# A transformer layer on one core: attention outputs turned by DMA instead of TensorE, output projection one segment later, residual rows loaded into the partial sums

## The chip, the core and the metric

The kernel runs on 1 core of one Trainium2 chip (trn2). The metric is the device time in microseconds (us). Times before: 3125.69 us, median of 3 runs (3119.35 to 3127.86).

## The reference

The input x is (16, 512, 256) in 32-bit floats: 16 batches of 512 tokens of width 256. One pre-norm layer is computed:

```python
def attn(inputs):                       # 32 query heads, 16 key/value heads, width 64
    qkv = inputs @ W_qkv                # 256 -> 2048 + 1024 + 1024
    scores = einsum('bhqd,bhkd->bhqk', q, repeat(k, 2)) / sqrt(64)
    scores = scores + alibi_slope[h] * (key_pos - query_pos)
    scores = where(causal, scores, -inf)
    out = einsum('bhqk,bhkd->bhqd', softmax(scores), repeat(v, 2))
    return out.reshape(B, S, 2048) @ W_out
def ffn(x):                             # 256 -> 64 -> 1024 -> 64 -> 256
    return (gelu((x @ U1) @ V1 + b1) @ U2) @ V2 + b2
x = x + attn(layernorm(x))
x = x + ffn(layernorm(x))
```

## The kernel before

**Numbers.** TensorE multiplies 16-bit floats, so nearly every operand is kept as two 16-bit halves: a high half (ScalarE rounds the value to 16 bits) and a low half (the rest, by VectorE where the value is in PSUM, by GpSimd where it is in SBUF). A product is three matmuls: low by high, high by low, high by high (`split_mm`, L437 through `mm`).

**Loops.** The outer loop runs over the 16 batches (`body(i, mode)`); the code of a body is written once for the first batch (FIRST), once as a hardware loop over the 15 others (MID), and once more as a tail (LAST) that finishes what is still in the pipe. A body has 16 steps `s`, one for each key/value head with its two query heads, and a step has 5 segments `n`. Each engine walks through the same steps and segments in a fixed order written by hand, and the engines are tied together by counting semaphores. The stages of a head are spread over several steps:

- step s: q of head s is projected (segment 1 or 2), k of a pair of heads in segment 0 of odd steps, v in segment 4 of steps 0 to 3 and 8 to 11. SyncE's DMA queue (SP) copies the halves to where the scores need them; `k_pair` copies are L394, L395 and L398, `q_pair` copies L406, L407 and L410.
- step s + 2: the row maxima of the scores, one block a segment (`max_scores` on TensorE, `maxima` on VectorE, L914). The key copies have to be there.
- step s + 7 (ATT): the scores again, one block a segment, transposed; ScalarE takes the exponential into `p_f` (L730, three buffers) and rounds it to `p_hi` (L688), GpSimd takes the low half `p_lo` (L1063). The high and low halves of segment n are made in segment n + 1, so those of segment 4 are made in segment 0 of the next step.
- step s + 8, segments 1 and 3: `attend`, the product with v for each of the two query heads into `o_acc`. The first waits for all five `p_lo` of the head. VectorE divides by the sum (`normalise`, L928 and L933) into `o_f`, 128 rows x (4 tiles x 128) in 32-bit floats.
- step s + 9, segment 0: `transpose_o`, four 128x128 transposes of `o_f` on TensorE into the PSUM bank `transposes` (L559). ScalarE rounds it into `ot[0]` (`o_t_hi`), VectorE takes `ot[1]` (`o_t_lo`, L837). `ot` is a ring of 8 heads.
- steps 12 to 15 and 0 to 11, segment 3 (OUT_SEG): `project_out`, 12 matmuls for one tile of 128 tokens and a group of 4 heads (a group takes 4 steps, one tile each). VectorE adds the result to `x_acc` (`add_out`, L921); the first group adds it to `x_residual`, the last one writes `x_rows`.
- steps 8 to 11: statistics of the second layer norm (L992 to L997, right after `add_out` in segment OUT_SEG), with the power on GpSimd (L1076) in segment 4; the feed-forward part follows up to step 15, its hidden layer in steps 13 and 14.
- after step 7, VectorE does the first layer norm of the next batch (`ln1`), with a power on GpSimd (L1046).

Projections share two PSUM banks in turn (`projection_order`, `next_proj`). SP's own order in a step: maxima (every fourth step), k copies (odd steps), q copies; the residual rows at s = 2, the next batch's rows at s = 4.

Of the kernel before, what the change touches and what calls it, by code (L numbers as in the profile page):

```python
# [28 lines left out]
P = 128  # L29
# [33 lines left out]
MAX_SEG, K_SEG, V_SEG = 1, 0, 4  # L63

OUT_RING, OUT_GROUP, OUT_LAG, OUT_SEG = 8, 4, 12, 3
# [83 lines left out]
MULTIPLES = (1, 2, 4, 8, 16, 32, 64, 80, 192)  # L149
# [60 lines left out]
def layer(nc, x, w_qkv, w_out, u1, v1, b1, u2, v2, b2, k_aug, q_aug, ident_d, ident_b_d, causal_d, out):  # L210
    B = x.shape[0]
    ctx = ExitStack()
    with ctx:
# [34 lines left out]
        o_f = sb("o_f32", [P, T, 2 * HD], F32)  # L248
        rden = sb("rden", [P, 2, T], F32)
        ot = [sb(f"o_t_{p}", [P, OUT_RING, S], F16) for p in ("hi", "lo")]  # L250
# [8 lines left out]
        xres = sb("x_residual", [P, T, D], F32)  # L259
# [25 lines left out]
        xres_in, y_out = sem("xres_in"), sem("y_out")  # L285
# [9 lines left out]
        hi_q, hi_k, hi_v, hi_ot, hi_m = sem("hi_q"), sem("hi_k"), sem("hi_v"), sem("hi_ot"), sem("hi_m")  # L295
# [4 lines left out]
        max_done, lo_q, lo_k, lo_v, lo_ot, lo_m = sem("max_done"), sem("lo_q"), sem("lo_k"), sem("lo_v"), sem("lo_ot"), sem("lo_m")  # L300
# [42 lines left out]
        def _(sp):  # L343
# [28 lines left out]
            def body(i, mode):  # L372
                for s in range(KV):
# [56 lines left out]
        def _(pe):  # L430
# [31 lines left out]
            def body(i, mode):  # L462
# [688 lines left out]
```

## Time and profile before

| | |
|---|---|
| median of 3 runs | 3125.69 us |
| profiled execution, its own time | 3124.16 us |
| its span, first to last instruction | 3122.4 us |
| TensorE (PE) busy | 2834.3 us, 91% |
| VectorE (DVE) busy | 2240.8 us, 72% |
| ScalarE (ACT) busy | 2167.0 us, 69% |
| GpSimd (POOL) busy | 1729.3 us, 55% |
| mean share of the DMA engines, all queues | 26.5% |
| mean granted TensorE clock | 0.987 |

One batch takes 188.6 us in the middle of the run: the scores of step 0 start at 1500.70 us and again at 1689.28 us. A matmul's busy time overlaps that of the next, so on TensorE the distance from one start to the next is what an instruction costs. In brackets at the end of a timeline row stands the idle time ahead of it and what ended it; "issue" is idle time that ended with nothing that the profile shows.

### The profile page before, as it was taken

To read this page: it belongs to the slowest core of one execution; us is meant where nothing else is said; L and a number is where in the kernel's file an instruction comes from. 1 tells how busy PE (TensorE), PEld (TensorE's weight loads), DVE (VectorE), ACT (ScalarE), POOL (GpSimd) and SP (SyncE) were. 2 spreads that over 40 slices of the span, in tenths; PEclk is the share of its full clock that TensorE was granted. 3 is DMA by queue.
4 is the path that set the end of the run, shared out by engine and by line. 5 is a ranking of instruction groups with operands and counts; after the bars stand their busy time and mean duration, and the time that the engine had idled before them with its cause. 6 is when DMAs were issued, how large, how long until landed. Compare 5 with 4: busy or idle time off the path is not lost.

```text
span 3122.4 us, 99572 instructions
## 1 busy us (share of the span) xinstructions
PE 2834.3 (91%) x32328; PEld 1975.6 (63%) x32328; DVE 2240.8 (72%) x7035; ACT 2167.0 (69%) x3828; POOL 1729.3 (55%) x1560
## 2 busy tenths in 40 slices
PE   4899999989989899899999999899898998999986
PEld 1576666766657566666766667666575666666664
DVE  6777677776767777677776777767677776777763
ACT  2676767667677676767767676676776767677683
POOL 1555555555555555555555555555555555555564
PEclk9999999999999999999999999999999999999997
DMA  6232232322223222232322323222232222323210
GB/s 167 64 72 55 56 73 48 79 53 64 62 54 77 48 67 60 56 74 46 78 54 55 74 47 78 54 63 62 54 77 48 67 60 56 74 48 78 55 36 8
DMA packets 220087, 195.25 MB, mean 63 GB/s; under 512 B 41738, under 2 KB 217866, under 8 KB 219274
## 3 DMA queue, kind: packets, MB, share of 16 engines
q1 hardware_dynamic: 219540, 188.32, 25.6%
q8 instruction: 299, 4.90, 0.7%
q14 instruction: 248, 2.03, 0.2%
HBM read 27.73 MB, written 8.39 MB: 12 GB/s over the span
## 4 chain that ended last, share of the span: by engine, by line
PE 30%; issue 28%; POOL 26%; ACT 5%; DVE 5%; POOLq 1%; DVEq 0%; ACTq 0%
POOL p_lo L1063 25%; PE proj L437 13%; PE scores L437 6%; PE o_acc L437 5%; PE max_scores L437 2%; PE ffn_acc L437 2%; ACT h_f L810 1%; ACT L730 1%; DVE max_scores L914 1%; DVE v_lo L837 1%; DVE x_rows L855 1%; ACT p_f L730 1%; ACT L810 1%; PE transposes L559 1%; POOL h_lo L1086 1%
## 5 line engine op out<-in xcount | busy, mean ns | idle before, releaser
L1063 POOL TENSOR_TENSOR p_lo<-p_f,p_hi 128x512 f16<-128x512 f32 x1280 | 1474.1, 1158 | 1103.1 <-ACT p_hi L688 1101.0
L730 ACT ACTIVATE p_f<-scores 128x512 f32<-128x512 f32 x1280 | 756.0, 591 | 432.3 <-PE scores L437 303.7
L688 ACT ACTIVATE p_hi<-p_f 128x512 f16<-128x512 f32 x1280 | 802.3, 627 | 53.4 <-issue 37.1
L914 DVE CUSTOM_DVE_ANT_0 max_scores<-max_scores,causal 128x384 f32<-128x384 f32 (+3 forms) x1184 | 564.2, 508 | 281.9 <-PE max_scores L437 279.5
L437 PE MATMUL scores<-q_hi_lo,k_lo_hi 128*128 128x512 f16 (+3 forms) x2048 | 614.7, 300 | 30.5 <-issue 30.2
L437 PE MATMUL scores<-q_hi_aug,k_hi_aug 128*128 128x512 f16 (+3 forms) x2048 | 587.4, 300 | 0.0
L437 PE MATMUL o_acc<-v_hi_one,p_lo 128*128 128x65 f16 x5120 | 521.3, 195 | 44.7 <-POOL p_lo L1063 44.6
L437 PEld LDWEIGHTS o_acc<-v_hi_one,p_lo 128*128 128x128 f16 x5120 | 473.7, 98 | 81.4 <-issue 42.3
L437 PE MATMUL o_acc<-v_lo,p_hi 128*128 128x64 f16 x5120 | 521.2, 194 | 0.0
L437 PE MATMUL o_acc<-v_hi_one,p_hi 128*128 128x65 f16 x5120 | 521.1, 195 | 0.0
L437 PEld LDWEIGHTS o_acc<-v_lo,p_hi 128*128 128x128 f16 x5120 | 470.5, 99 | 19.7
L437 PEld LDWEIGHTS o_acc<-v_hi_one,p_hi 128*128 128x128 f16 x5120 | 470.5, 98 | 0.0
L437 PE MATMUL scores<-ident_bf,causal 128*128 128x128 bf16 x2048 | 449.5, 220 | 0.0
L914 DVE CUSTOM_DVE_ANT_0 ffn_acc<-ffn_acc,causal 128x384 f32<-128x384 f32 (+2 forms) x864 | 413.9, 509 | 34.8 <-PE ffn_acc L437 33.6
L437 PE MATMUL max_scores<-k_hi_aug,q_hi_aug 96*128 96x384 f16 (+3 forms) x1184 | 284.0, 301 | 77.6 <-DVE row_max L914 74.1
L437 PE MATMUL proj<-xn_t_hi,wqkv_lo 128*128 128x512 f16 x768 | 294.4, 383 | 28.8 <-DVE v_lo L837 27.3
L437 PE MATMUL proj<-xn_t_lo,wqkv_hi 128*128 128x512 f16 x768 | 293.5, 382 | 0.0
L437 PE MATMUL proj<-xn_t_hi,wqkv_hi 128*128 128x512 f16 x768 | 293.3, 382 | 0.0
L437 PE MATMUL proj<-wo_hi,o_t_lo 128*128 128x256 f16 x1024 | 284.6, 278 | 2.6 <-DVE o_t_lo L837 1.5
L914 DVE DVE_READ_ACCUMULATOR2_ANT row_max<- 128x1 f32 x2048 | 284.8, 139 | 1.3
L437 PE MATMUL proj<-wo_hi,o_t_hi 128*128 128x256 f16 x1024 | 284.7, 278 | 0.0
L437 PE MATMUL proj<-wo_lo,o_t_hi 128*128 128x256 f16 x1024 | 284.2, 278 | 0.0
(110 smaller groups left out, 5212.0 us busy)
## 6 DMA issues: line engine op xcount, KB each, us to landing
q_hi_aug<-q_pair_hi SPq DMA_DIRECT2D x512, 64.0 KB, 2.0
q_hi_lo<-q_pair_hi SPq DMA_DIRECT2D x512, 64.0 KB, 2.0
q_hi_lo<-q_pair_lo SPq DMA_DIRECT2D x512, 64.0 KB, 2.0
k_hi_aug<-k_pair_hi SPq DMA_DIRECT2D x256, 64.0 KB, 2.0
k_lo_hi<-k_pair_hi SPq DMA_DIRECT2D x256, 64.0 KB, 2.0
k_lo_hi<-k_pair_lo SPq DMA_DIRECT2D x256, 64.0 KB, 2.0
x_rows<-in_L_attn_inputs SPq DMA_DIRECT2D x17, 512.0 KB, 3.8
x_residual<-in_L_attn_inputs SPq DMA_DIRECT2D x16, 512.0 KB, 3.8
```

Source lines behind the costliest of these rows:

```text
L437: return nc.tensor.matmul(out_ap, lhs, rhs, start=start, stop=stop, skip_group_check=True)
L559: last = nc.tensor.transpose(bank[:, qt * P:(qt + 1) * P], o_f[:, qt, :], ident[:, :])
L688: return nc.scalar.activation(out_ap, in_ap, ACT.Copy, scale=scale)
L730: nc.scalar.activation(p_f[:, k % 3, :], score_bank[k % 2][:, :], ACT.Exp).then_inc(exp_done, 1)
L810: nc.scalar.activation(h_f[:, c % 2, :], proj("h", c)[:, :], ACT.Gelu_apprx_tanh, bias=b1c[:, c:c + 1], scale=1.0 / FFN_SCALE).then_inc(ge ...
L837: return nc.vector.scalar_tensor_tensor(out=out_ap, in0=bank, scalar=scale, in1=high, op0=ALU.mult, op1=ALU.subtract)
L855: last = nc.vector.tensor_scalar(xt[:, t, :], xt[:, t, :], agg[:, t, 0:1], rstd[:, t:t + 1], ALU.subtract, ALU.mult)
L914: last = nc.vector.tensor_tensor_reduce(out=bank, in0=bank, in1=causal[:, (T - 1 - qt) * P:S], scale=1.0, scalar=-3e38, op0=ALU.add, op1=A ...
L1063: nc.gpsimd.tensor_tensor(p_lo[:, slot, n, :], p_f[:, k % 3, :], p_hi[:, slot, n, :], ALU.subtract).then_inc(lo_p, 1)
L1086: nc.gpsimd.tensor_tensor(h_lo[:, c % 2, :], h_f[:, c % 2, :], h_hi[:, c % 2, :], ALU.subtract).then_inc(lo_h, 1)
```

## The change

- `transpose_o` on TensorE, the rounding of its PSUM result (`o_t_hi`, ScalarE, step s + 9, segment 0) and the low half from PSUM (`o_t_lo`, VectorE) are gone.
- ScalarE now rounds `o_f` itself, before the transpose, into `o_hl[:, slot, 0]`, in step s + 8, segment 4 (O_SEG), after waiting for the second `normalise` of that step, which is in segment 3. `o_f` and `o_hl` have two slots.
- GpSimd takes the low half of `o_f` into `o_hl[:, slot, 1]` in step s + 9, segment 0, ahead of the `p_lo` of segment 4.
- SP issues one DMA transpose a head (128 rows x 1024 16-bit values, both halves) into `ot`. It stands in SP's list in step s + 8 after the q copies and waits for the low half, so SP gets past it in step s + 9. `project_out` waits for the DMAs of its group.
- `project_out` and `add_out`, with the layer-norm statistics behind them, move from segment 3 to segment 4.
- `x_residual` is gone. The residual rows are loaded straight into `x_acc`, in four DMAs of one tile each in steps 10 to 13, and the first `add_out` adds to `x_acc` in place.

```diff
-MAX_SEG, K_SEG, V_SEG = 1, 0, 4
+MAX_SEG, K_SEG, V_SEG, O_SEG = 1, 0, 4, 4
-OUT_RING, OUT_GROUP, OUT_LAG, OUT_SEG = 8, 4, 12, 3
+OUT_RING, OUT_GROUP, OUT_LAG, OUT_SEG = 8, 4, 12, 4
...
@@ SP
-                    if s == 2 and mode != LAST:
-                        if 16 * i - OUT_LAG > 0:
-                            sp.wait_ge(acc_done, at(16 * i - OUT_LAG))
-                        sp.dma_start(xres[:, :, :], x_src(i.value())).then_inc(xres_in, 16)
+                    if in_stage(mode, s, ATT + 1):
+                        slot, kv = s % 2, (s - ATT - 1) % KV
+                        sp.wait_ge(lo_o, at(g - ATT))
+                        sp.sem_inc(gate, 1)
+                        sp.dma_start_transpose(ot[:, kv % OUT_RING, :, :].rearrange("p a (t q) -> p (a t) q", q=P),
+                                               o_hl[:, slot, :, :].rearrange("p a q -> p (a q)")).then_inc(ot_in[slot], 16)
+                    if s in range(OUT_LAG - 2, OUT_LAG + 2) and mode != LAST:
+                        t = s - (OUT_LAG - 2)
+                        if 16 * i + t - 3 > 0:
+                            sp.wait_ge(acc_done, at(16 * i + t - 3))
+                        sp.dma_start(xacc[:, t, :], x_src(i.value())[:, t, :]).then_inc(xres_in[t], 16)
@@ TensorE
-                def transpose_o(s):
-                    a = i * KV + s - ATT - 2
-                    bank = transposes_bank(lo_ot, a + 1)
-                    pe.wait_ge(o_done, at(2 * (a + 1)))
-                    for qt in range(T):
-                        last = nc.tensor.transpose(bank[:, qt * P:(qt + 1) * P], o_f[:, qt, :], ident[:, :])
-                    last.then_inc(pe_ot, 1)
...
                     if t == 0:
-                        pe.wait_ge(lo_ot, at(16 * i + s - OUT_LAG + OUT_GROUP))
+                        for slot in range(2):
+                            pe.wait_ge(ot_in[slot], at(16 * (8 * i + (s - OUT_LAG) // 2 + 2)))
@@ ScalarE
-                        if n == out_segment(s) and in_stage(mode, s, ATT + 2):
-                            a = g - ATT - 2
-                            act.wait_ge(pe_ot, at(a + 1))
+                        if n == O_SEG and in_stage(mode, s, ATT + 1):
+                            a, slot = g - ATT - 1, s % 2
...
-                            copy(ot[0][:, a_slot(s) % OUT_RING, :], t_bank[:, :]).then_inc(hi_ot, 1)
+                            act.wait_ge(o_done, at(2 * (a + 1)))
+                            copy(o_hl[:, slot, 0, :], o_f[:, slot, :, :].rearrange("p t c -> p (t c)")).then_inc(hi_o, 1)
@@ VectorE
                     if h == 0:
-                        if a > 0:
-                            dve.wait_ge(pe_ot, at(a))
+                        if a > 1:
+                            dve.wait_ge(lo_o, at(a - 1))
...
-                        if n == out_segment(s) + out_lag(s) and in_stage(mode, s, ATT + 2):
-                            dve.wait_ge(hi_ot, at(g - ATT - 1))
-                            low(ot[1][:, a_slot(s) % OUT_RING, :], t_bank[:, :], ot[0][:, a_slot(s) % OUT_RING, :],
-                                1.0).then_inc(lo_ot, 1)
...
-                                if t == 0:
-                                    dve.wait_ge(xres_in, at(16 * (i + 1)))
-                                add_out(xacc, s, xres)
+                                dve.wait_ge(xres_in[t], at(16 * (i + 1)))
+                                add_out(xacc, s, xacc)
@@ GpSimd
                     for n in range(SEG):
+                        if n == 0 and in_stage(mode, s, ATT + 2):
+                            slot = (s - ATT - 2) % 2
+                            pool.wait_ge(hi_o, at(i * KV + s - ATT - 1))
+                            nc.gpsimd.tensor_tensor(o_hl[:, slot, 1, :], o_f[:, slot, :, :].rearrange("p t c -> p (t c)"),
+                                                    o_hl[:, slot, 0, :], ALU.subtract).then_inc(lo_o, 1)
                         if n > 0 and in_stage(mode, s, ATT):
                             low_p(SEG * (i * KV + s - ATT) + n - 1, s % 2, n - 1, SEG * s + n - 1)
```

## Rows read from the trace of the kernel before

**Rows 1.** The page: busy time of the engines.
```profile
PE 2834.3 (91%) x32328; PEld 1975.6 (63%) x32328; DVE 2240.8 (72%) x7035; ACT 2167.0 (69%) x3828; POOL 1729.3 (55%) x1560
```

**Rows 2.** TensorE's timeline in one batch: four of its 12 idle stretches.
```profile
1586.29 0.19 PE L437 MATMUL o_acc<-v_hi_one,p_lo 128*128 128x65 f16 x1 [2.36 <-POOL p_lo L1063]
...
1609.98 0.60 PE L530 MATMUL proj<-ident,row_max 128*8 128x128 f32 x4 [0.80 <-DVE v_lo L837]
...
1635.30 0.39 PE L437 MATMUL proj<-xn_t_hi,wqkv_lo 128*128 128x512 f16 x1 [0.51 <-DVE v_lo L837]
...
1689.28 0.39 PE L437 MATMUL scores<-q_hi_lo,k_lo_hi 128*128 128x512 f16 x1 [2.16 <-issue]
```

**Rows 3.** TensorE's timeline: the transposes of step 0 and the next block.
```profile
1501.42 0.60 PE L559 MATMUL transposes<-ident,o_f 128*128 128x128 f32 x4
1501.86 0.38 PE L437 MATMUL scores<-q_hi_lo,k_lo_hi 128*128 128x512 f16 x1
```

**Rows 4.** Groups by line: count, then busy us, mean ns of one, idle before.
```profile
L1063 POOL TENSOR_TENSOR p_lo<-p_f,p_hi 128x512 f16<-128x512 f32 x1280 | 1474.1, 1158 | 1103.1 <-ACT p_hi L688 1101.0
L688 ACT ACTIVATE p_hi<-p_f 128x512 f16<-128x512 f32 x1280 | 802.3, 627 | 53.4 <-issue 37.1
...
L837 DVE SCALAR_TENSOR_TENSOR o_t_lo<-transposes,o_t_hi 128x512 f16<-128x512 f32 x256 | 176.4, 689 | 49.5 <-ACT o_t_hi L688 39.4
...
L559 PE MATMUL transposes<-ident,o_f 128*128 128x128 f32 x1024 | 154.2, 273 | 1.5 <-DVE o_f L933 1.1 <-DVE xn_t_lo L837 0.4
...
L688 ACT ACTIVATE o_t_hi<-transposes 128x512 f16<-128x512 f32 x256 | 152.3, 595 | 7.2 <-PE transposes L559 7.2
```

**Rows 5.** Timeline, step 0 to 1: last `p_lo` and the `attend` behind it.
```profile
1512.07 1.16 POOL L1063 TENSOR_TENSOR p_lo<-p_f,p_hi 128x512 f16<-128x512 f32 x1 [2.83 <-ACT p_hi L688]
...
1513.74 0.20 PE L437 MATMUL o_acc<-v_hi_one,p_lo 128*128 128x65 f16 x1
```

**Rows 6.** TensorE's and GpSimd's timelines, steps 8 and 9.
```profile
1591.13 0.28 PE L437 MATMUL proj<-wo_hi,o_t_lo 128*128 128x256 f16 x1
1592.44 0.19 PE L437 MATMUL o_acc<-v_hi_one,p_lo 128*128 128x65 f16 x1
1593.35 0.27 PE L437 MATMUL scores<-q_hi_lo,k_lo_hi 128*128 128x256 f16 x1
1594.12 0.38 PE L437 MATMUL proj<-wqkv_hi,xn_t_lo 128*128 128x512 f16 x1
...
1594.91 0.54 POOL L1076 TENSOR_TENSOR rstd<-var_eps,nhalf 128x1 f32<-128x1 f32 x1 [1.78 <-DVE var_eps L997]
...
1598.57 0.20 PE L437 MATMUL o_acc<-v_hi_one,p_lo 128*128 128x65 f16 x1
```

**Rows 7.** The same two timelines, steps 14 and 15.
```profile
1662.91 0.60 PE L530 MATMUL proj<-ident,row_max 128*8 128x128 f32 x4 [0.55 <-ACT h_f L810]
...
1673.98 3.39 POOL L1063 TENSOR_TENSOR p_lo<-p_f,p_hi 128x512 f16<-128x512 f32 x3
...
1677.78 0.20 PE L437 MATMUL o_acc<-v_hi_one,p_lo 128*128 128x65 f16 x1
```

**Rows 8.** TensorE's timeline in the tail (LAST), one of seven alike.
```profile
3044.69 0.20 PE L437 MATMUL o_acc<-v_hi_one,p_lo 128*128 128x65 f16 x1 [1.17 <-POOL p_lo L1063]
```

**Rows 9.** DMA: the queue (packets, MB, share), issues (KB each, us to landing).
```profile
q1 hardware_dynamic: 219540, 188.32, 25.6%
...
q_hi_aug<-q_pair_hi SPq DMA_DIRECT2D x512, 64.0 KB, 2.0
...
x_residual<-in_L_attn_inputs SPq DMA_DIRECT2D x16, 512.0 KB, 3.8
```

**Rows 10.** Timelines, SP in step 5 and TensorE at the start of step 6.
```profile
1555.18 0.48 SPq L394 DMA_DIRECT2D k_hi_aug<-k_pair_hi  x1
...
1557.69 1.17 SPq L398 DMA_DIRECT2D k_lo_hi<-k_pair_lo  x2
...
1562.20 0.38 PE L437 MATMUL max_scores<-k_hi_aug,q_hi_aug 96*128 96x512 f16 x1
```

More of the change, by code:

```diff
@@ L146 @@
 PROJ = {use: k % 2 for k, use in enumerate(projection_order())}
-MULTIPLES = (1, 2, 4, 8, 16, 32, 64, 80, 192)
+MULTIPLES = (1, 2, 4, 8, 16, 32, 64, 80, 128, 192)
 FREE = 1
@@ L247, in layer @@
         p_lo = sb("p_lo", [P, 2, SEG, 512], F16)
-        o_f = sb("o_f32", [P, T, 2 * HD], F32)
+        o_f = sb("o_f32", [P, 2, T, 2 * HD], F32)
+        o_hl = sb("o_hi_lo", [P, 2, 2, S], F16)
         rden = sb("rden", [P, 2, T], F32)
-        ot = [sb(f"o_t_{p}", [P, OUT_RING, S], F16) for p in ("hi", "lo")]
+        ot = sb("o_t", [P, OUT_RING, 2, S], F16)
+        ot_half = [ot[:, half * OUT_RING // 2:(half + 1) * OUT_RING // 2, :, :] for half in range(2)]
+        staged_wo = [o.rearrange("p r a b -> p (r a b)").bitcast(F32).rearrange("p (c n) -> p c n", n=D) for o in ot_half]
         mcol = sb("row_max", [P, 2, T, 8], F32)
@@ L284, in layer @@
         zeroed, qaug_in, x_in, k_rows = sem("zeroed"), sem("qaug_in"), sem("x_in"), sem("k_rows_set")
-        xres_in, y_out = sem("xres_in"), sem("y_out")
+        xres_in, y_out = [sem(f"xres_in{t}") for t in range(T)], sem("y_out")
         qdup_in = [sem(f"qdup_in{r}") for r in range(RING)]
@@ L351, in _ @@
             for half in range(2):
-                sp.dma_start(ot[half][:, :, :].rearrange("p a b -> p (a b)").bitcast(F32).rearrange("p (c n) -> p c n", n=D),
+                sp.dma_start(staged_wo[half],
                              w_out[half * KV // 2 * P:(half + 1) * KV // 2 * P, :].rearrange("(c p) n -> p c n", p=P)).then_inc(w_in[2], 16)
@@ L581, in project_out @@
                     if t == 0:
-                        pe.wait_ge(lo_ot, at(16 * i + s - OUT_LAG + OUT_GROUP))
+                        for slot in range(2):
+                            pe.wait_ge(ot_in[slot], at(16 * (8 * i + (s - OUT_LAG) // 2 + 2)))
                     for k in range(OUT_GROUP):
                         kv = OUT_GROUP * group + k
-                        last = split_mm(bank[:, 0:D], [o[:, kv % OUT_RING, t * P:(t + 1) * P] for o in ot],
+                        last = split_mm(bank[:, 0:D], [ot[:, kv % OUT_RING, part, t * P:(t + 1) * P] for part in range(2)],
                                         [w[:, kv, :] for w in wo], k == 0, k == OUT_GROUP - 1)
@@ L704, in _ @@
             for half in range(2):
-                last = copy(wo[0][:, half * KV // 2:(half + 1) * KV // 2, :],
-                            ot[half][:, :, :].rearrange("p a b -> p (a b)").bitcast(F32).rearrange("p (c n) -> p c n", n=D), WO_SCALE)
+                last = copy(wo[0][:, half * KV // 2:(half + 1) * KV // 2, :], staged_wo[half], WO_SCALE)
             last.then_inc(split_hi, 1)
@@ L866, in _ @@
                 low(wqkv[1][:, c, :], src, wqkv[0][:, c, :], W_SCALE).then_inc(split_done, 1)
-            staged_wo = [o[:, :, :].rearrange("p a b -> p (a b)").bitcast(F32).rearrange("p (c n) -> p c n", n=D) for o in ot]
             small = p_hi[:, :, :, :].rearrange("p a b c -> p (a b c)").bitcast(F32)
@@ L929, in normalise @@
                     if h == 0:
-                        if a > 0:
-                            dve.wait_ge(pe_ot, at(a))
+                        if a > 1:
+                            dve.wait_ge(lo_o, at(a - 1))
                     dve.wait_ge(recip_done, at(2 * a + h + 1))
-                    nc.vector.tensor_tensor(o_f[:, :, h * HD:(h + 1) * HD], o[:, :, 0:HD],
+                    nc.vector.tensor_tensor(o_f[:, (s - ATT - 1) % 2, :, h * HD:(h + 1) * HD], o[:, :, 0:HD],
                                             rden[:, h, :].unsqueeze(2).to_broadcast([P, T, HD]),
```

23 lines of the change are left out of this document (9 added, 14 removed).

## The prediction

> **What bounds the kernel now.** I read the page first, then the groups by line, then TensorE's timeline through one batch, and last the timelines of the other engines at each place where TensorE's rows show idle time or come close to it. The page says that TensorE is busy 91% of the span and no other engine above 72% [rows 1]. The timeline says the same more sharply: in a batch of 188.58 us (the scores of step 0 to those of the next batch) TensorE's idle stretches are 12 rows with 13.9 us together, the first at 1586.29 and the last at 1689.28, and the rest is matmuls issued back to back [rows 2]. Three kinds of places matter here. Step 8 (2.36 us, and more behind it) is the first layer norm of the next batch. Steps 10, 11 and 12 each have a stall of 0.5 to 1.2 us for `v_lo`, of which the first and the last are shown. And 2.16 us go at the loop's end. So work taken from TensorE is worth its full issue time in most steps, and nothing in a step where a stall stands behind it.
>
> **What is removed.** Four transposes of `o_f` stand between two blocks for 1501.86 - 1501.42 = 0.44 us [rows 3]. (The group's busy time, 154 us for 1024, counts overlaps; the issue distance is 256 x 0.44 = 113 us.) In a batch that is 16 x 0.44 = 7.04 us. VectorE loses 256 x 0.689 = 176 us; ScalarE swaps a copy of 595 ns for one like `p_hi`, 627 ns; GpSimd gets 256 more of 1.16 us, 297 us or 65% busy in all [rows 4]. On none of the three is that a throughput limit; where it lies in the order is what counts.
>
> **Where the 0.44 us is not gained.**
>
> - Steps 10, 11, 12: the transposes stand ahead of a stall that ends with VectorE's `v_lo`, which hangs on the v projection and not on the transposes. The stall grows by what is taken away: -3 x 0.44 = -1.32. The `v_lo` chain itself I leave as long as it is: `add_out` and the statistics now come into it, but VectorE idled near there, and it loses `o_t_lo`.
> - Step 14: the stall ends with ScalarE's gelu [rows 7], whose queue holds the same work: -0.44.
> - Step 8: VectorE's `ln1` starts after `add_out` instead of before it, but segment 4 of step 7 starts 1.31 us earlier, since `project_out` follows it. I count the 0.44 as gained and 0.4 on top: +0.4.
> - Steps 1, 3 and 4: the last `p_lo` ends at 1513.23 and `attend` starts at 1513.74, 0.51 later [rows 5]. In step 8, where TensorE does wait, the start comes 0.23 after the end of `p_lo` (1584.90 + 1.16 = 1586.06 in the same timeline), so the slack is 0.28, and 0.16 of each 0.44 is lost: -0.5. The new low half of `o` doesn't add to it here: its input is there when segment 4's exponential is, and the v projection (1.3 us) and the moved `project_out` (1.31 us, 1591.13 to 1592.44 [rows 6]) run meanwhile. That is the cover; without it 1.16 us would be late in each step. In steps 5 to 7 the moved projection alone covers it, with some 0.2 us to spare by the same reckoning.
> - Step 9: GpSimd's power of the layer norm waits for VectorE's statistics, which now follow `project_out` in segment 4. Before, it starts 1594.91 - 1592.44 = 2.47 after the last output matmul. Now, from the start of the scores of segment 4: 0.77 (1593.35 to 1594.12) + 1.31 + 2.47 + 0.54 for the power, + 1.16 for the new low half, + 1.16 for the last `p_lo`, + 0.23 = 7.64. `attend` would be free to start after 5.22 (1593.35 to 1598.57) + 1.31 - 0.44 = 6.09 [rows 6]. Lost: -1.55. Steps 10 to 12 have at least 1.6 us more between the same two points and hide it.
> - Step 15: GpSimd comes out of the feed-forward low halves late and does three `p_lo` in a row, to 1677.37, and `attend` follows at 1677.78 [rows 7]. The new low half goes ahead of the third: `attend` starts at about 1677.37 + 1.16 + 0.23 = 1678.76, 0.98 later than before instead of 0.44 earlier: -1.42.
>
> Sum of a batch: 7.04 - 1.32 - 0.44 + 0.40 - 0.50 - 1.55 - 1.42 = 2.2 us. Some 15.5 batches have this cover (15 and steps 9 to 15 of the first): 34 us. In the tail nothing covers GpSimd: seven steps already wait 1.17 us for `p_lo` [rows 8], and each gets the rounding and the low half (0.6 + 1.16) less the 1.31 of `project_out` that now runs under them: I take +0.7 x 7 = +5. At the very end the last transpose is awaited by the last output projection, once: +3. Net -26.
>
> **The DMA transposes.** No row shows one. It moves 256 KB. Landing, from below: between 64 KB in 2.0 us and 512 KB in 3.8 us, so 2.8 us [rows 9]. The queue's packets take 25.6% x 16 x 3122.4 / 219540 = 58 ns each; if pieces are rows of 128 values (256 bytes), 1024 pieces take 1024 x 58 ns / 16 = 3.7 us of all engines; if they are 16 values long, 8192 take 30 us, the upper bound, which would fill the queue. I take 3.7 us, nearest to pieces like those the queue has now (1 KB rows), and about 5.5 us to landing. `project_out` needs it only in every fourth step, some 7 us or more after the low half. What else stands behind: SP's copies of k. In step 5 the first is issued at 1555.18 and the last ends issuing at 1558.86; it lands at 1560.9, and the maxima of step 6 start at 1562.20, so 1.3 us to spare; the transpose is issued some 1.8 us ahead of the first copy [rows 10]. So up to 3.1 us of issue, or 1.8 + 3.7 + 1.3 = 6.8 us in the rings, cost nothing. Issue of a copy is 0.6 us; eight such (one a block) would be 4.8 us and cost 1.7 us in steps 5 and 7, 16 batches: +54. I take one to three: 0.
>
> Here the Trainium skill speaks on both sides. Its page Advanced Engine Details and Errata, section X-Bar Transpose (TRN2), calls transposing DMAs as fast as ordinary ones; by that the price is 0, as above. No row here shows one.
>
> **Residual rows.** Four issues for one, 0.4 us each on SP, two steps (over 20 us) ahead of their use against a landing of 3.8 us or less [rows 9]; `add_out` costs the same in place. 0.
>
> **Forecast.** On the profiled execution's own 3124.16 us (span 3122.4), less 26: 3098. The median of the runs is 1.5 higher: 3099.
>
> **Rivals.**
>
> - *All of it is gained* (chance 0.12): the stalls above are shorter than I reckon since VectorE has 0.69 us a step less. 113 less 8 of the tail: 3125.7 - 105 = 3020. For it: many stalls end with VectorE. Against: steps 9 and 15 hang on GpSimd.
> - *GpSimd's new low half lies in the path* (0.13): VectorE gives `o_f` late, ScalarE, waiting for it in segment 4, is late with the rounding and with `p_hi` behind it, and GpSimd starts the new operation when it would have started the last `p_lo`. Then `attend` comes 1.16 - 0.28 = 0.88 later than before in 15 steps of 16 batches: +211, 3337. It decides from the point where more than 0.28 us of the 1.16 is exposed on the mean. For it: VectorE is at 72% and in bursts behind. Against: it loses 0.69 us a step, and the projection in segment 4 gives 1.31.
> - *The transposes fill the DMA queue* (0.11): the engines are 25.6% busy, 3.1 us of a 12.2 us step; a transpose of over 9.1 us makes them the bound. With pieces of 32 values, 4096 x 58 ns / 16 = 14.9 us, a step takes 14.9 + 3.1 = 18.0, and the kernel 256 x 18.0 + 60 for the ends = 4670; at 30 us, 8,500. For it: no row shows into how many pieces a transpose falls. Against: the row length of the data alone gives 3.7 us, and what stays under some 7 us costs nothing. It decides from there.
> - *Moved stalls eat all* (0.06): steps 0 to 7 lose their gain too, 3116 to 3135.
>
> The Trainium skill's page VectorE: DVE Perf Modes, section The three transpose paths, gives 1309 ns for a 128x128 block of 16-bit values by DMA. If eight such blocks add up, my estimate by that page is 10.5 us a transpose, the third rival's case at 256 x 13.6 + 60 = 3540; no row here shows it.
>
> **How the numbers follow.** The likeliest case has 0.58, with a range of its own of 3070 to 3120: the stalls of steps 9 and 15 may be absent (-47) or the small slacks of steps 5 to 7 gone (+20). About 0.3% (9 us) is what a measurement of this kernel can tell from no change. Faster: 0.54 + 0.12 = 0.66; same: 0.04 of the first case, 0.02 of the second rival's, 0.06 of the last: 0.12; slower: 0.11 + 0.11 = 0.22. The range reaches down to the first rival and up into the light cases of the second (less than half of the 1.16 us exposed): 3020 to 3150, with 0.01 left out below and 0.18 above.
>
> **What would show it.** The rows of L559, `o_t_hi` and `o_t_lo` are gone, and TensorE's busy time is down by some 110. Idle time ahead of `o_acc`, ended by `p_lo`, appears in steps 9 and 15 and not elsewhere. The transpose's row says its landing; wrong if above 7 us, or if TensorE waits for k copies or in `project_out` for a DMA. Wrong the other way if idle time in steps 10 to 12 doesn't grow. The second rival shows as idle time of TensorE before `o_acc` in nearly every step, with ScalarE waiting for `o_f`.

## The result

The kernel with the change takes 3190.22 us (median of 4 runs, 3179.89 to 3200.06) against 3123.95 us before (4 runs): ratio 1.0212, 95% interval 1.0174 to 1.0251. It is slower by 66 us, where 26 us less were forecast. Spans of the profiled executions: 3192.9 and 3122.4 us, mean granted clock 0.974 and 0.987.

The page of the kernel after, engines, queue and groups, answering to [rows 1, 4, 9]:

```profile
PE 2775.3 (87%) x31304; PEld 1868.7 (59%) x31304; DVE 2080.0 (65%) x6779; ACT 2183.6 (68%) x3828; POOL 2015.4 (63%) x1816
...
q1 hardware_dynamic: 490644, 255.46, 38.2%
...
L1046 POOL TENSOR_TENSOR p_lo<-p_f,p_hi 128x512 f16<-128x512 f32 x1280 | 1475.6, 1160 | 817.9 <-ACT p_hi L675 815.7
...
L1054 POOL TENSOR_TENSOR o_hi_lo<-o_f,o_hi_lo 128x512 f16<-128x512 f32 x256 | 295.6, 1155 | 14.1 <-ACT o_hi_lo L675 11.8
...
x_acc<-in_L_attn_inputs SPq DMA_DIRECT2D x64, 128.0 KB, 2.3
```

TensorE does less (2775 for 2834 us) in a longer span, so its idle time has grown. The view of waits (engine, line and tile that waited, what ended the wait; us in total, times, longest) says for what:

```profile
PE max_scores L433 <- DVE row_max L902: 80.6, 65, 2.7
PE o_acc L433 <- POOL p_lo L1046: 71.0, 38, 3.4
PE scores L433 <- issue: 50.4, 14, 4.8
PE proj L433 <- DVE v_lo L826: 41.4, 32, 1.7
PE proj L433 <- DVE x_acc L909: 39.8, 45, 1.1
```

In the kernel before, the same view has 74.1, 44.6, 30.2, 27.3 and 5.0 us. What stands out is the wait for `x_acc`, the sum that `add_out` writes: before, it was 0.34 us once a batch, in step 13. Another 9.4 us of it stand before the turning of the row maxima (L526). The loop's end ("issue") costs 20 us more, `p_lo` 26 us more. The transposes themselves are hardly to be seen: TensorE waits for one of them once in the whole run, 3.4 us.

Where in a batch it went. Step lengths (from one step's first scores to the next's), kernel after less kernel before. The measured column is one batch in the middle of each run (1528.36 to 1722.74 and 1500.70 to 1689.28), the last column the mean of the 14 batches from the first loop end to the tail:

| steps | forecast, us | measured, us | mean of 14, us |
|---|---|---|---|
| 0 | -0.44 | +1.21 | +1.22 |
| 1 to 4 | -1.28 | +2.22 | +2.22 |
| 5 to 7 | -1.32 | -1.31 | -1.34 |
| 8 | -0.84 | 0.00 | +0.18 |
| 9 | +1.11 | +0.24 | +0.24 |
| 10 to 12 | 0 | 0.00 | +0.36 |
| 13 | -0.44 | +0.10 | +0.10 |
| 14 | 0 | +0.73 | +0.73 |
| 15 | +0.98 | +2.61 | +1.30 |
| batch | -2.23 | +5.80 | +5.0 |

The one batch shown has the longest idle stretch of the run at its end (4.84 us in step 15, where the mean is 3.60), and no stretch at the low clock in steps 8 and 11, where some of the others have one.

Over the 14 batches the mean is 194.13 for 189.13, +5.0 us: 70 us. The tail got 3.4 us longer and the start 3.0 shorter, which makes the 70.5 us between the spans.

Steps 1 to 4. Timelines of TensorE and VectorE:

```profile
1541.46 0.39 PE L433 MATMUL proj<-xn_t_hi,wqkv_lo 128*128 128x512 f16 x1 [1.12 <-DVE x_acc L909]
...
1553.50 0.60 PE L526 MATMUL proj<-ident,row_max 128*8 128x128 f32 x4 [0.63 <-DVE x_acc L909]
```

```profile
1540.38 0.69 DVE L826 SCALAR_TENSOR_TENSOR v_lo<-proj,v_hi_one 128x512 f16<-128x512 f32 x1 [2.26 <-ACT v_hi_one L675]
1540.99 0.41 DVE L909 SCALAR_TENSOR_TENSOR x_acc<-proj,x_acc 128x256 f32<-128x256 f32 x1
```

In segment 4, VectorE does `v_lo` first and `add_out` behind it, though the matmuls of `project_out` ended before those of v. VectorE stands idle for 2.26 us until ScalarE has rounded v, so the PSUM bank of `project_out` comes free at 1541.4, and TensorE, which needs that bank for its next projection, waits 1.12 us. Before, `add_out` stood in segment 3.

Steps 15 and 0, the loop's end:

```profile
1716.66 0.27 PE L433 MATMUL proj<-v_hi,h_hi 128*128 128x256 f16 x1
1717.07 0.28 PE L433 MATMUL proj<-v_hi,h_lo 128*128 128x256 f16 x1
...
1717.63 0.27 PE L433 MATMUL proj<-v_hi,h_hi 128*128 128x256 f16 x1
1722.74 0.60 PE L433 MATMUL scores<-q_hi_lo,k_lo_hi 128*128 128x512 f16 x1 [4.84 <-issue]
```

```profile
1716.60 0.41 DVE L909 SCALAR_TENSOR_TENSOR x_acc<-proj,x_acc 128x256 f32<-128x256 f32 x1
```

`project_out` of step 15 stands directly ahead of the last projection of the feed-forward part (12 matmuls in two banks). Its second bank waits for `add_out`: 0.30 us at 1717.07. Then 4.84 us pass to the scores of the next body, 2.16 before [rows 2]. From the last projection's first matmul to the first scores the mean is 5.39 us, before 3.63; from there to the first `attend` 4.35 us, before 3.16 with 0.44 of transposes in it. The view by stretches shows why the second grew:

```profile
1718.00:1720.00 2.00, 0.00 (x0) 0.00 (x0) 0.63 (x1) 0.34 (x1) 1.15 (x1) 1.00 1.39 110
1720.00:1722.00 2.00, 0.00 (x0) 0.00 (x0) 0.00 (x0) 0.00 (x0) 0.00 (x0) 0.67 0.88 58
1722.00:1724.00 2.00, 1.26 (x4) 0.54 (x5) 0.00 (x0) 0.01 (x1) 0.00 (x0) 0.50 0.84 284
```

The columns are the stretch, its length, busy us of PE, PEld, DVE, ACT and POOL, then the granted clock, DMA share and GB/s. After the long idle stretch TensorE works at 0.50, the level of 1.2 GHz; before, the clock is 1.00 in every such stretch around 1689, and it is so behind all 14 ends. In the kernel after it falls to 0.50 at 13 of the 14 ends, at 9 of them only some matmuls behind the first scores, which still take 0.39 us. The batch before this one shows the fall; the same matmul takes 0.38 us at full clock:

```profile
1528.36 0.39 PE L433 MATMUL scores<-q_hi_lo,k_lo_hi 128*128 128x512 f16 x1 [3.28 <-issue]
...
1530.00 0.63 PE L433 MATMUL proj<-xn_t_hi,wqkv_lo 128*128 128x512 f16 x1
```

Steps 8 and 9. TensorE's waits and GpSimd's timeline in step 8:

```profile
1616.68 0.19 PE L433 MATMUL o_acc<-v_hi_one,p_lo 128*128 128x65 f16 x1 [3.41 <-POOL p_lo L1046]
```

```profile
1613.14 1.02 POOL L1029 TENSOR_TENSOR rstd<-var_eps,nhalf 128x4 f32<-128x4 f32 x1 [2.74 <-DVE var_eps L841]
1614.13 1.15 POOL L1054 TENSOR_TENSOR o_hi_lo<-o_f,o_hi_lo 128x512 f16<-128x512 f32 x1
1615.24 3.52 POOL L1046 TENSOR_TENSOR p_lo<-p_f,p_hi 128x512 f16<-128x512 f32 x3
```

The wait is 3.41 us for 2.36 before [rows 2]: GpSimd stood in the power of the layer norm, and the new low half goes ahead of the `p_lo` that TensorE waits for.

### The profile page after: what moved, and what is told of

Same layout as the page of the kernel before. It is cut to its first block, busy times and chain, and to the rows that moved or that the text cites. A ratio compares the mean times of both kernels' runs of the same rounds, so it can differ in the third digit from the quotient of the medians.

```text
span 3192.9 us, 98277 instructions
## 1 busy us (share of the span) xinstructions
PE 2775.3 (87%) x31304; PEld 1868.7 (59%) x31304; DVE 2080.0 (65%) x6779; ACT 2183.6 (68%) x3828; POOL 2015.4 (63%) x1816
## 3 DMA queue, kind: packets, MB, share of 16 engines
q1 hardware_dynamic: 490644, 255.46, 38.2%
## 4 chain that ended last, share of the span: by engine, by line
POOL 34%; issue 28%; PE 28%; ACT 5%; DVE 4%; POOLq 1%; DMA 1%; DVEq 0%; ACTq 0%; SPq 0%
POOL p_lo L1046 28%; PE proj L433 13%; PE scores L433 6%; PE o_acc L433 5%; POOL o_hi_lo L1054 5%; PE max_scores L433 2%; PE ffn_acc L433 2%; ACT h_f L799 1%; ACT L716 1%; DVE v_lo L826 1%; ACT p_f L716 1%; POOL h_lo L1074 1%; ACT L799 1%; DVE max_scores L902 1%; POOLq L308 1%
## 5 line engine op out<-in xcount | busy, mean ns | idle before, releaser
L433 PE MATMUL scores<-q_hi_lo,k_lo_hi 128*128 128x512 f16 (+3 forms) x2048 | 623.8, 305 | 50.7 <-issue 50.4
L433 PE MATMUL scores<-q_hi_aug,k_hi_aug 128*128 128x512 f16 (+3 forms) x2048 | 598.6, 305 | 0.0
L433 PE MATMUL proj<-wo_hi,o_t 128*128 128x256 f16 x2048 | 383.3, 275 | 3.4 <-DMA o_t<-o_hi_lo 3.4
L433 PE MATMUL proj<-xn_t_hi,wqkv_lo 128*128 128x512 f16 x768 | 300.0, 391 | 82.7 <-DVE v_lo L826 41.4
L1054 POOL TENSOR_TENSOR o_hi_lo<-o_f,o_hi_lo 128x512 f16<-128x512 f32 x256 | 295.6, 1155 | 14.1 <-ACT o_hi_lo L675 11.8
L675 ACT ACTIVATE q_pair_hi<-proj 128x512 f16<-128x512 f32 x256 | 152.3, 595 | 201.7 <-PE proj L433 201.6
```

Of the source, the lines that this page charges most:

```text
L433: return nc.tensor.matmul(out_ap, lhs, rhs, start=start, stop=stop, skip_group_check=True)
L675: return nc.scalar.activation(out_ap, in_ap, ACT.Copy, scale=scale)
L1054: nc.gpsimd.tensor_tensor(o_hl[:, slot, 1, :], o_f[:, slot, :, :].rearrange("p t c -> p (t c)"), o_hl[:, slot, 0, :], ALU.subtract).then_i ...
```

## The experiments

The edits are to the kernel after, unless said otherwise. Ratios are to the kernel before. "Last projection to first scores" is counted from the first of the last projection's 12 matmuls, as above.

**e1, `add_out` ahead of `v_lo` in VectorE's segment 4.**

```diff
-    v_lo of this segment
     q_pair_lo, k_pair_lo, ...
     add_out(...)
+    v_lo of this segment
```

> The changed kernel with one edit: VectorE does add_out (and the statistics behind it) ahead of v_lo in segment 4 of the steps with a v projection. Theory A (VectorE's order): in the changed kernel add_out stands behind v_lo, which waits for the v projection, so the PSUM bank of the output projection comes free late, and TensorE waits for x_acc at the start of the next k, q or maxima block, 49 us in 60 rows. Then these rows vanish and the time falls by 40 to 50 us, to about 3143. Rival (GpSimd in the path): the stall only moves to the next wait, the attend behind p_lo, and the time stays within 10 us of 3190.

Measured: 3139.11 us, ratio 1.0048 (1.0032 to 1.0065). The waits for `x_acc` are gone, and steps 1 to 4 are 3.8 us a batch shorter. The loop's end stays: 5.40 us from the last projection to the first scores, and 4.74 us from there to the first `attend`, 0.4 more than in the kernel after, since the clock stands at 0.50 for longer. Gain 51 us, as Theory A had it.

**e2, e3, e6: what stands in the DMA queue at the loop's end.** e2 holds the transpose of step 15 until TensorE's first scores of the next body, e3 does so on top of e1, e6 holds the output's store on top of e1.

```diff
+    sp.wait_ge(pe_scores, first scores of the next body)
     sp.dma_start_transpose(...)        # e2, e3
     sp.dma_start(out[...], x2)         # e6
```

> The changed kernel with one edit: the DMA transpose that is issued at the end of a body (head 7, step 15) is held until TensorE has run the first scores block of the next body. Theory B (loop end): this transpose is in the DMA rings when the engines fetch the code of the loop's start; it makes TensorE idle longer (from the last ffn matmuls to the first scores 5.39 us on the mean of 14 ends against 3.63 before), and behind the longer gap the clock is 0.5 for some us (first scores to first attend 4.32 us against 3.16). Then the two fall back to about 3.6 and 2.7, worth 3.4 us an end, 45 to 50 us in all: 3142. Rival (the output store's DMA or VectorE's last work set the gap): no change, within 10 us of 3190.

> Both edits of the two kernels before. If the two causes are apart, the gains add up: about 3190 - 47 - 48 = 3095, some 30 us faster than the kernel before the change, near what the prediction's sum gave (3099). If the second rival (GpSimd's low half in the path) holds, it stays above 3160.

> The kernel of e1 with one edit on SP: the store of the finished batch at a body's end is held until TensorE has run the first scores block of the next body. Theory D: the store (512 KB) is in the DMA rings while TensorE's code is fetched; held back, the idle time at the loop's end falls from 3.6 to about 2.4 us or less and the clock stays up: some 1.2 + 1.8 us at 15 ends, 45 us: 3094. If the fetch doesn't meet the store: within 8 us of 3139.

Measured: e2 3279.07 us, 1.0507 (1.049 to 1.0525); e3 3222.12, 1.0303 (1.0267 to 1.0339); e6 3141.07, 1.0054 (1.0038 to 1.0069). In e2 and e3 the held transpose ended up behind the copies of q, and `project_out` of step 0 waited for it:

```profile
PE proj L440 <- DMA o_t<-o_hi_lo: 62.2, 17, 4.6
```

So their times say little, but the stretch in question does: from the last projection to the first scores it is 5.09, 5.22 and 5.36 us, for 5.39. Neither the transpose nor the store, each held alone, makes the gap; my expectations of 3142, 3095 and 3094 us all failed.

**e4, the segment alone: the kernel before with OUT_SEG = 4.**

```diff
-OUT_RING, OUT_GROUP, OUT_LAG, OUT_SEG = 8, 4, 12, 3
+OUT_RING, OUT_GROUP, OUT_LAG, OUT_SEG = 8, 4, 12, 4
```

> The kernel before with one part of the change alone: the output projection and add_out in segment 4 instead of 3; transposes on TensorE as before. Theory A: the same wait for x_acc appears, 60 rows, +40 to +50 us, less what VectorE's o_t_lo (still there) adds on top: about 3170. Rival: the segment is neutral and the cost of the change lies in the DMA and on GpSimd: 3115 to 3135.

Measured: 3216.33 us, 1.0296 (1.0279 to 1.0314), 46 us more than I expected. The move alone, with VectorE's order as it was, costs 93 us without any DMA transpose. Per batch, on the mean, steps 1 to 4 take 2.2 us more than before, just as in the change; steps 13 and 14 take 1.8 more, steps 15 and 0 3.3 more. The last projection to the first scores is 4.76 us, on to `attend` 5.30. So the gap at the loop's end comes in the main with the move. Waits of TensorE:

```profile
PE scores L437 <- issue: 45.5, 14, 3.8
...
PE proj L437 <- DVE x_acc L921: 20.5, 30, 0.7
```

**e5, e1 with the projection of step 15 back in segment 3.**

```diff
+def out_seg(s):
+    return 3 if s in (15,) else 4
```

> The kernel of e1 (add_out ahead of v_lo) with the output projection of step 15 alone back in segment 3. Theory C (bank at the loop end): in segment 4 the projection stands directly ahead of the last ffn matmuls, whose second bank waits 0.3 to 0.4 us for add_out, so TensorE reaches the loop's branch late and its idle time there and the low clock behind it follow. Then last ffn matmuls to first scores falls from 5.4 us to about 3.7, first scores to first attend from 4.7 to 2.7, 3.5 us an end, 50 us in all: 3090. Rival D (the output store's 512 KB in the DMA rings during the code fetch) without C: less than 10 us gained.

Measured: 3099.83 us, 0.9919 (0.9903 to 0.9936). Last projection to first scores 3.46 us, on to `attend` 3.70. Its loop's end in TensorE's timeline:

```profile
1673.98 0.27 PE L437 MATMUL proj<-v_hi,h_hi 128*128 128x256 f16 x1
1676.56 0.39 PE L437 MATMUL scores<-q_hi_lo,k_lo_hi 128*128 128x512 f16 x1 [2.31 <-issue]
```

The 12 matmuls run without a break, the idle stretch is 2.31 us, and the clock falls behind 2 of the 14 ends, where it fell behind 13 in the kernel after. Gain over e1: 39 us. Something new takes part of it back: at 12 places TensorE stands idle ahead of the first `attend` of step 0, ended by "issue" (9.3 us in all); what for, the profile does not say.

Where the gap grows can be narrowed further. At each of the 14 ends one DMA packet of 16 KB of the queue q8, of the kind `instruction`, starts ahead of the first scores. On the mean it starts 3.16 us ahead of them in the kernel after and 3.08 before; over all 18 kernels these means lie between 2.9 and 3.3 us. What differs is how late it starts: 2.23 us after the last projection's first matmul in the kernel after, 2.22 in e1 and 1.90 in e4, but 0.55 in the kernel before and 0.49 in e5. So of the 1.76 us by which the stretch grew, 1.68 lie ahead of this packet and next to nothing behind it. That fits a TensorE which comes late to the loop's end, as Theory C has it. For which engine the packet is meant the trace does not say.

**e7, the whole projection in segment 3.**

```diff
-... OUT_SEG = 8, 4, 12, 4
+... OUT_SEG = 8, 4, 12, 3
```

> The changed kernel with one part undone: output projection and add_out in segment 3 as before; DMA transposes, GpSimd's low half and the residual rows as changed. If the segment is what costs (e4: +94 us alone), this is faster than the kernel before: 113 less what GpSimd's low half exposes without the projection's cover. In steps 4 to 7 and 12 to 15 the last p_lo would then be late for attend by 0.5 to 1 us, in the others little: 3124 - 113 + 60 = 3070. Rival (GpSimd's low half is the cost and segment 4 its cover): 3190 or more, with idle time before o_acc in every step.

Measured: 3141.6 us, 1.0058 (1.0039 to 1.0078), not the 3070 that I expected. Both new waits are away (`x_acc` 5.0 us, "issue" before the scores 27.9), but:

```profile
PE o_acc L433 <- POOL p_lo L1046: 118.9, 81, 3.9
```

This is the second rival, in part: without the 1.31 us of `project_out` in segment 4 the low half lies in TensorE's path, with 0.78, 0.20, 0.77 and 1.10 us in steps 5, 6, 7 and 15 of each batch, and 3.86 in step 8.

**e8, e1 with segment 3 at steps 13 and 15, transpose and store of the body's end held.**

> Built from both theories of the loop end: e1's order, the output projection in segment 3 in steps 13 and 15 and in 4 elsewhere, and at a body's end both the transpose of head 7 and the store held until TensorE has run the first scores of the next body. If C and D are both right, the loop end costs less than in the kernel before: 3139 - 50 - 12 (the wait for q_pair_lo in step 13) - 10 = 3065. If neither is: 3125 or more.

Measured: 3098.44 us, 0.9921 (0.9904 to 0.9938); e5 and no more, where I expected 3065. Step 13 is 0.54 us shorter than in e5, step 14 0.37 longer.

**e9, e10, e13, e14: GpSimd's order.** GpSimd does the last `p_lo` before the low half of `o`: in e9 on top of e7, in e10 on top of e8's segments (nothing held), in e13 as e10 with the transpose of odd steps behind the key copies, in e14 as e10 in steps 8 and 9 alone.

```diff
 for n in range(SEG):
-    if n == 0: low half of o, then_inc(lo_o)
     if n > 0: low_p(...)
     if n == 0: low_p of segment 4
+    if n == 0: low half of o, then_inc(lo_o)
```

> The change with the output projection and add_out back in segment 3 (as e7_seg3, 3141.6 us, 119 us of TensorE idle time before o_acc ended by p_lo), and GpSimd does the last p_lo of a head before the low half of o instead of behind it. Theory G: what e7 loses is the 1.16 us of the low half standing ahead of the last p_lo. Then the idle time ended by p_lo falls from 119 us to about the 43 us of the kernel before, and the time to about 3141.6 - 76 = 3066 us, range 3050 to 3090. Rival G2: GpSimd's load, not its order, is late (65% busy; the low half then pushes the p_lo behind it instead); then the idle time moves to row_max or to the next o_acc and the time stays above 3120. Rival G3: the transposes, issued 1.2 us later, make SP's k copies late: idle time before max_scores with a DMA as its end, and 3100 or more.

> The change with add_out ahead of v_lo in VectorE's segment 4, the projection in segment 3 at steps 13 and 15 only (as e8_all without its holding of SP's DMAs at the body's end; 3098.4 us), and GpSimd does the last p_lo before the low half of o. Theory G: the stalls for p_lo of step 8 (3.4 us against 2.4 before) and step 9 (0.5 to 0.8) lose the 1.16 us, some 1.5 us a batch: 3098 - 25 = 3073 us, range 3060 to 3085. Rival G2: in segment 4 the projection covers the low half already and the stall of step 8 hangs on the layer norm alone: within 6 us of 3098. Against e9 it says which segment is the better one once GpSimd's order is right: if both theories hold e9 is the faster by up to 10 us, since v_lo isn't behind the projection.

> e10_seg3_13_15_plo_first (3101.2 us) with one more edit: the transpose that SP comes to in an odd step stands behind that step's key copies instead of ahead of them. Theory H: e10's 25 us of waits before max_scores for k_lo_hi go, and 8 us for o_t stay or go; time 3101 - 25 = 3076 us, range 3068 to 3088. Rival H2: the waits for k_lo_hi only stand in the place of waits for row_max, which grow by as much; then 3095 to 3101, and the time that the low half costs lies with VectorE's maxima of step 8.

> e8_all's order of segments, no DMA held (3098.4 us), GpSimd does the last p_lo before the low half of o in steps 8 and 9 alone, where TensorE waited for it. Theory H: step 8's wait of 3.4 us for p_lo loses up to 1.1 us and step 9's 0.5 goes, and SP's delay concerns one odd step only: 3098.4 - 15 x 1.5 = 3076 us. Rival H2: the wait in step 8 moves to row_max behind it, which ends with VectorE after the layer norm; only step 9's 0.5 us is gained: 3091 us, range 3088 to 3098.

Measured: e9 3190.08 us, 1.0206 (1.0183 to 1.0229); e10 3101.24, 0.9935 (0.9922 to 0.9949); e13 3089.27, 0.9887 (0.9871 to 0.9904); e14 3088.52, 0.9884 (0.9867 to 0.99). My expectation for e9 (3066) missed by 124 us, in the way of rival G3, and that for e10 (3073) by 28, with the time that G2 gave. Waits of e9, then of e10:

```profile
PE max_scores L433 <- DVE row_max L902: 86.9, 54, 2.5
PE max_scores L433 <- DMA k_lo_hi<-k_pair_lo: 55.4, 39, 2.5
PE proj L433 <- DMA o_t<-o_hi_lo: 55.2, 33, 6.0
...
PE o_acc L433 <- POOL p_lo L1046: 39.7, 51, 3.0
```

```profile
PE max_scores L437 <- DVE row_max L906: 106.9, 69, 2.7
...
PE o_acc L437 <- POOL p_lo L1050: 31.6, 20, 2.0
...
PE max_scores L437 <- DMA k_lo_hi<-k_pair_lo: 25.0, 40, 1.8
```

The waits for `p_lo` shrink as meant (118.9 to 39.7 us; 71.1 in e8 to 31.6). In their place TensorE waits for the key copies, since these stand behind the transpose in SP's list, and the transpose behind the low half. SP in e10:

```profile
1561.68 1.38 SPq L408 DMA_TRANSPOSE o_t<-o_hi_lo  x1
1563.11 0.51 SPq L382 DMA_DIRECT2D k_hi_aug<-in_k_aug  x1
...
1566.25 1.17 SPq L391 DMA_DIRECT2D k_lo_hi<-k_pair_lo  x2
```

e13 takes that queue away (waits for the key copies 25.0 to 1.8 us) and gains 12 us, between Theory H and rival H2: 9 us come back as waits for `p_lo` (31.6 to 40.4), and those for `row_max` stay at 106.9, 32 more than in e8. e14 measures the same from the other side: 10 us under e8. They come from step 9, which is 0.67 us shorter. In step 8 the wait for `p_lo` is down from 3.41 to 2.25 us, but the waits for `row_max` behind it grow by 32 us over the run, and the step is 0.25 us longer. This is rival H2.

**e11, e5 with GpSimd's low half cut to 8 of 512 columns.** The rest of the low half of the attention output is left out.

> e5_seg3_at15 (3099.8 us) with GpSimd's low half of o cut to 8 of 512 columns; the rest of the low half of the attention output is left out of the computation (it stays zero). Everything else, the transposing DMAs too, is the same. It measures what the 1.16 us of the low half cost in all, whatever the order. Theory G: 1.5 us a batch in steps 8 and 9 and up to 5 us in the tail: 3099.8 - 28 = 3072 us, and e10 is within 10 us of it. Rival G2 (GpSimd's load matters beyond the order): 3050 or less, and e10 stays well above. Rival: the low half costs nothing (covered by the projection): 3095 to 3100.

Measured: 3068.66 us, 0.9822 (0.9808 to 0.9835). The low half on GpSimd costs 31 us in e5, as Theory G gave (3072 expected). By order alone I had 10 us (e14 under e8).

**e12, e15, e16: the other parts in the kernel before.** e12 is e5's order with TensorE's transposes kept. It put `v_lo` behind `o_t_lo` in steps 10 to 12 too, which was not meant; e15 has it where the kernel before has it there. e16 loads the residual rows into `x_acc` and changes nothing else.

```diff
+if n == V_SEG: v_lo behind add_out     # e15; e12 in every segment
-sp.dma_start(xres, ...)                # e16: one load, step 2
+sp.dma_start(xacc[:, t, :], ...)       # e16: four, steps 10 to 13
```

> The kernel before, TensorE's transposes and the x_residual load kept, with the projection in segment 4 except step 15 (segment 3 there), and add_out ahead of v_lo in VectorE's segment 4: the mended move alone. e4_seg4_alone, the move not mended, took 3216. If the mended move is neutral it takes 3124, and the transposes by DMA with the residual rows are worth 3099.8 - 3124 = -24 us net in e5. If the mended move still costs (v_lo and the layer norm behind the projection), it takes 3140 to 3165, and the DMA transposes are worth -40 to -65. If it gains (cover for p_lo), 3100 to 3115, and the transposes are worth little. My theory: 3140, since v_lo's stalls of steps 10 to 12 still grow by 1.3 us of projection less what VectorE had to spare.

> e12_before_seg4_mended (3203.6 us) with its side effect taken out: there VectorE took v_lo behind o_t_lo in steps 10 to 12 too, and the waits for v_lo grew from 2.53 to 4.91 us a batch. Here v_lo stands behind add_out in segment 4 alone and is where it was elsewhere. Theory I: the move of the projection to segment 4, mended, costs 3203.6 - 15 x 2.4 - 3124 = +44 us with TensorE's transposes kept (3168 us, range 3155 to 3180), and the transposes by DMA bring 3099.8 - 3168 = -68 us on top of it. Rival I2: the move is then free and this takes 3120 to 3140, so that the DMA transposes bring -20 to -40 only. Rival I3: v_lo's waits stay (they hang on the projection in segment 4, not on o_t_lo): 3195 or more.

> The kernel before with the residual rows loaded into x_acc in four loads in steps 10 to 13, and nothing else of the change. The forecast priced this part at 0: 3124 us, range 3115 to 3133. Rival: the four loads (0.4 us each on SP, behind a wait for the add_out of the tile in steps 10 to 13) hold up the copies of q and k behind them; then waits of max_scores for a DMA, and more than 3133. If below 3115, the 512 KB load at step 2 had been in somebody's way.

Measured: e12 3203.59 us, 1.0262 (1.0248 to 1.0276); e15 3146.46, 1.0077 (1.0065 to 1.0089); e16 3122.59, 1.0 (0.9991 to 1.0009). e12 is 57 us slower than e15 for one VectorE operation of 0.69 us that came too early in three steps. (I had expected 3140 for e12 and 3168 for e15, so the move costs less than Theory I and more than rival I2 said.) Waits for `v_lo` before the v projection in e12 and in e15:

```profile
PE proj L441 <- DVE v_lo L841: 53.7, 32, 2.4
```

```profile
PE proj L441 <- DVE v_lo L841: 27.3, 32, 1.2
```

That wait and the one before the turning of the maxima (25.8 and 12.6 us) make 40 of the 57 us. The other 17 go with the clock. In e12, step 11 takes 15.8 us instead of 14.1 in 6 of 14 batches, with the clock at 0.50 around the wait of 2.01 us for `v_lo`; in e15 it takes 13.35 in all of them. Step 8 takes 16.1 instead of 14.5 us, or nearly so, in 6 of 14 batches, in e15 in 2.

The runs in one table, us:

| projection in | TensorE's transposes | DMA transposes | difference |
|---|---|---|---|
| segment 3 | 3122.9 (before) | 3141.6 (e7) | +19 |
| segment 4, as in the change | 3216.3 (e4) | 3190.2 (after) | -26 |
| segment 4, mended (`add_out` ahead of `v_lo`, step 15 in segment 3) | 3146.5 (e15) | 3099.8 (e5) | -47 |

## Why the prediction was wrong

**The step that failed** is the pricing of the moved `project_out` and `add_out`. I counted its matmuls as cover for GpSimd and its delay to the statistics in steps 8 and 9, and for steps 0 to 7 looked at nothing but `p_lo`. `add_out` also frees the bank of the projection. Two terms were missing:

- VectorE's order in segment 4: `add_out` behind `v_lo`, bank late, 3.3 us a batch in steps 1 to 4. Shown by e1: 51 us.
- The loop's end: `project_out` directly ahead of the last projection, which needs two banks. That its place is the cause is shown by e5, 39 us, and from the other side by e4. That the bank is the link is argued and not shown: the wait of 0.3 us at 1717.07 is seen in the row, and the `instruction` packet comes 1.7 us later than before, but no run has the late projection with an early bank. Why 0.3 us of waiting become 1.7 stays open; the transpose and the store on SP are not the cause (e2, e3, e6). The forecast had no term for the clock either, which is low behind 13 of the 14 ends.

With both mended the kernel takes 3099.8 us, the 3099 of the forecast. That agreement is partly luck, as the steps show (measured in the kernel after, in the one batch, unless said otherwise):

- **Removed, 7.04 us a batch.** Steps 5 to 7 gained 0.44 each, to the hundredth.
- **Steps 10 to 12** lost exactly what they gained, 0.00, as forecast: `v_lo` waits went from 27.3 + 12.6 to 41.4 + 19.6 us, 1.3 a batch. In 3 of the 14 batches, though, step 11 takes 15.02 us instead of 13.35, at a clock of 0.50 behind its wait of 1.65 us; before, in none.
- **Step 8** was to gain 0.84 and gained nothing. I took the cover of the v projection and `project_out` from steps 1 to 4; here GpSimd comes out of the power at 1614.13 with the low half ahead of `p_lo`, and nothing covers it. The wait grew by 1.05 us, and the one for `row_max` behind it shrank.
- **Step 9**, forecast to lose 1.55 by this very mechanism: the stall came and was 0.50 us. The direction was right, the size was not.
- **Step 15**: the stall on the third `p_lo` did not come. Instead steps 13 and 14 hold new waits for `q_pair_lo` (0.84) and `row_max` (1.36); I had step 14 down as no change and it lost 0.73. The first goes with the projection of step 13 in segment 3 (18.5 us in e5, 5.9 in e8), though a wait of 0.34 for `x_acc` comes in its place. The second is this row:

```profile
1703.07 0.39 PE L433 MATMUL max_scores<-k_hi_aug,q_hi_aug 96*128 96x384 f16 x2 [1.36 <-DVE row_max L902]
```

  It stands in all 14 kernels that have the projection of step 14 in segment 4, e4 and e15 with TensorE's transposes among them, and in none of the four that have it in segment 3 (before, e7, e9, e16). So it is a third price of the move that I put at nothing, and the mended kernels pay it too. It also hides the stall of step 15, as TensorE comes there later; in e7, which does not have it, the stall came:

```profile
1677.82 0.20 PE L433 MATMUL o_acc<-v_hi_one,p_lo 128*128 128x65 f16 x1 [1.10 <-POOL p_lo L1046]
```

- **Tail**: +3.4 us, forecast +8. The forecast's own terms for a step (0.6 + 1.16 - 1.31) give 0.45, not the 0.7 that I took.
- **DMA transposes**, priced 0: right as far as TensorE's waits tell. One lands in 3.1 us on the median (forecast 5.5), with 1.26 us of issue (under the 3.1 that I held free):

```profile
1692.50 1.26 SPq L404 DMA_TRANSPOSE o_t<-o_hi_lo  x1
```

```profile
o_t<-o_hi_lo SPq DMA_TRANSPOSE x256, 3.1
```

- **Residual rows**, priced 0: right (e16, 0.0 us).

**The rivals.** *All of it is gained*: no; the best arrangement found (e14) gains 35 us. *The low half in the path*: in step 8 and partly in e7, worth 31 us in e5 (e11), not 211. *The transposes fill the queue*: no. The queue has 490644 - 219540 = 271104 packets and 255.46 - 188.32 = 67.14 MB more, about 1059 packets of 248 bytes a transpose, so the pieces are in the main rows of 256 bytes; its engines worked (0.382 x 3192.9 - 0.256 x 3122.4) / 256 = 1.6 us more for each, where I took 3.7. *Moved stalls eat all* was nearest in kind, with 0.06; I had bounded it at 3135 by the gain of steps 0 to 7 and did not ask whether a moved operation could make a wait of its own.

The Trainium skill's page Advanced Engine Details and Errata, section X-Bar Transpose (TRN2), has transposing DMAs as fast as ordinary ones. By that rule 256 KB land between the 2.0 us of 64 KB and the 4.8 us of 512 KB (`x_rows`), and the trace agrees with 3.1. In the time of the DMA engines it agrees less: the 188.32 MB of the kernel before took 0.256 x 3122.4 us of all 16, which is 1.1 us for 256 KB, and a transpose takes 1.6. The Trainium skill's page VectorE: DVE Perf Modes, section The three transpose paths, gives 1309 ns for a block; these do not add up here, since eight blocks land in 3.1 us.

## What to carry to other kernels

When a matmul group is moved in a hand-written order, list for each engine what now stands between its last matmul and the operation that frees its PSUM bank; here the place of one operation on VectorE cost 51 us, more than the 47 that the DMA transposes brought in the mended order. Price a removal and a move apart: the same DMA transposes, with GpSimd's low half, were worth +19, -26 and -47 us by where the projection and `add_out` stood. And an operation put into the chain of a slow engine must be followed to the queue behind its result: e9 cured 79 us of one wait that e7 had and got 101 more of two others.

## What the runs showed of the hardware

- A DMA transpose of 128 rows x 1024 16-bit values between two SBUF tiles: 1.26 us of issue on SP, 3.1 us to landing on the median, about 1059 packets and 1.6 us of all 16 engines. The 64 KB copies around it did not slow down (still 2.0 us), the 512 KB load of `x_rows` did: 4.8 us to landing for 3.8 before (3.7 in e4 and e16, which have no DMA transposes).
- TensorE's clock at the loop's end. After 4.84 us of idle time it was granted 0.50 at the first scores. In the kernel before, after 2.16 us, it stayed at 1.00. The length alone does not decide: in e12, 1.98 us of idle time at the same place, the clock stayed full for the first matmuls and fell to 0.50 some 1.3 us later:

```profile
1734.00:1736.00 2.00, 1.32 (x9) 0.93 (x10) 0.00 (x0) 0.99 (x2) 0.28 (x1) 0.99 0.46 154
1736.00:1738.00 2.00, 2.00 (x8) 0.88 (x7) 1.77 (x6) 1.64 (x4) 1.64 (x2) 0.50 0.36 117
```

In e15 the first `attend` comes 4.8 us after the first scores in 9 of 14 iterations and 3.15 in the other 5, in the kernel before 3.16 in all. What tips it stays open; it is worth 1.1 us a batch, 15 of e15's 24 us over the kernel before. The low clock is not bound to the loop's end: in step 8 of the kernel before, with its waits of 2.36, 1.66 and 0.38 us, it comes in 6 of 14 batches, and the step then takes 16.4 to 16.6 us instead of 14.8; in the kernel after it comes in 10 of 14.
